# A graph-network kernel: sorting place pairs as one packed word instead of two float planes

## The reference

```python
edge_index = jnp.stack([src, dst])
x = _layernorm(x + _L0_gnn_ref(x, ...gate..., src, dst))           # tanh-gated sum of h[src] into dst
x = _layernorm(x + _L1_gnn_ref(x, edge_index, W1, ..., W2, ...))   # two attention layers, with self loops
x = _layernorm(x + _L2_gnn_ref(x, beta, src, dst))                 # here src is the row index: softmax over
                                                                   # cosine similarities, summed into src
x = _layernorm(x + _L3_gnn_ref(x, edge_index, edge_attr_64, ...))  # relu(x[src] + edge_attr @ Wl + bl) into dst
```

## Time and profile before

| | us |
|---|---|
| median of 3 runs (4032.59 to 4035.59) | 4035.1 |
| the profiled execution | 4035.14 |
| its span in the trace | 4033.3 |
| VectorE (DVE) busy, 5486 instructions | 2409.5 (60%) |
| GpSimd (POOL) busy, 2420 instructions | 2499.7 (62%) |
| TensorE (PE) busy, 5666 instructions | 1601.3 (40%) |
| ScalarE (ACT) busy, 3433 instructions | 1239.6 (31%) |
| part 1 of the sort on VectorE, from 900.47 | to 975.5 |
| part 2, from 1303.39 | to 1373.3 |
| part 3, from 1744.66 | to 1862.95 |

### The profile page before, as it was taken

The page is one execution under the profiler, slowest core; times in us unless marked ns, Lnnn a source line. Parts: engine busy times, 40 slices in busy tenths (PEclk is TensorE's granted clock), DMA queues, the critical chain, the costliest instruction groups (busy, mean ns, idle before and its releaser), DMA issues. The chain is left out here.

```text
span 4033.3 us, 34837 instructions
## 1 busy us (share of the span) xinstructions
PE 1601.3 (40%) x5666; PEld 1320.0 (33%) x5666; DVE 2409.5 (60%) x5486; ACT 1239.6 (31%) x3433; POOL 2499.7 (62%) x2420
## 2 busy tenths in 40 slices
PE   1988989977122156512552000000000277065221
PEld 1888888866122135301220000000000166054221
DVE  5565565549885977678985333348854234443554
ACT  1555555542232255402552222210000144033110
POOL 5777777777701774057602777770377677776777
PEclk9555555555555555556776555555555566566555
DMA  2555556655101244224642555540000155344000
GB/s 56 166 168 165 166 168 184 189 166 141 39 28 34 55 123 128 79 61 112 176 138 84 155 150 150 155 126 0 5 20 20 54 160 158 99 131 115 16 18 17
DMA packets 255330, 421.00 MB, mean 104 GB/s; under 512 B 79304, under 2 KB 86746, under 8 KB 255244
## 3 DMA queue, kind: packets, MB, share of 16 engines
q1 hardware_dynamic: 177932, 348.51, 28.0%
q0 software_dynamic: 77312, 71.64, 9.0%
HBM read 185.35 MB, written 236.81 MB: 105 GB/s over the span
## 5 line engine op out<-in xcount | busy, mean ns | idle before, releaser
L577 PE MATMUL banks<-node_w,x_t 65*125 65x200 f32 x1600 | 551.6, 536 | 0.0
L577 PEld LDWEIGHTS banks<-node_w,x_t 65*125 65x125 f32 x1600 | 514.9, 330 | 4.1
L224 POOL DMA_INDIRECT edge_rows<-x_rows,norm_s x400 | 413.9, 1035 | 144.8 <-issue 125.0
L790 PE MATMUL banks<-ident,cross_in 125*65 125x125 f32 (+4 forms) x26 | 11.2, 430 | 1236.4 <-DVE cross_in L813 848.0
L790 PEld LDWEIGHTS banks<-ident,cross_in 125*65 125x65 f32 (+4 forms) x26 | 3.9, 150 | 1242.1 <-DVE cross_in L813 850.4
L240 POOL DMA_INDIRECT x_rows<-r_x,src_scat_i x200 | 222.1, 1110 | 125.4 <-DVE r_x L2028 63.4
L240 POOL DMA_INDIRECT out_dram<-n_out,scat_i x200 | 222.5, 1112 | 80.1 <-issue 62.0
L620 DVE TENSOR_REDUCE n_var<-n_sq 125x8 f32<-125x512 f32 x125 | 85.6, 686 | 306.4 <-ACT n_sq L634 306.4
L224 POOL DMA_INDIRECT tops<-norm_rows,src_i x200 | 202.6, 1013 | 71.6 <-issue 68.8
L224 POOL DMA_INDIRECT edge_rows<-x_rows,key_i x200 | 199.0, 995 | 77.2 <-issue 60.7
L240 POOL DMA_INDIRECT norm_rows<-edge_rows,scat_i x200 | 205.4, 1027 | 66.6 <-issue 63.3
(11 more groups left out here) (455 smaller groups left out, 5230.2 us busy)
## 6 DMA issues: line engine op xcount, KB each, us to landing
h_rows<-r_h SPq DMA_DIRECT2D x125, 462.0 KB
x_rows<-r_x SPq DMA_DIRECT2D x125, 241.5 KB
x_rows<-r_x SPq DMA_DIRECT2D x125, 224.0 KB
r_x<-x_rows SPq DMA_DIRECT2D x125, 224.0 KB
x_rows<-n_out SPq DMA_DIRECT2D x125, 224.0 KB
n_in<-in_x_dram SPq DMA_DIRECT2D x100, 224.0 KB
x_mixed_edge_rows<-e_dup SPq DMA_DIRECT2D x50, 448.0 KB
n_c<-x_rows SPq DMA_DIRECT2D x100, 224.0 KB
```

The source lines that it names most:

```text
L224: g.indirect_dma_start(out=to[:, j, :], out_offset=None, in_=table, in_offset=bass.IndirectOffsetOnAxis(ap=idx[:, j:j + 1], axis=0)).then_ ...
L577: done = pe.matmul(product[h][:, n // 2, n % 2, :], x_t[u][:, at:at + P], node_w[:, :], start=True, stop=True)
L790: pe.transpose(crossings["bank"][0:cols, 0:rows], frm, ident[0:rows, 0:rows]).then_inc(s_tout, 1)
```

## The change

The key and its companion are packed in one 32-bit word, and the words are sorted as floats, in one plane. The key plus 256 (and plus 768 more from 64768 on) is shifted up by 15 bits, and the companion stands in the low 15 bits. The offsets keep the exponent field clear of its lowest and highest values. Keys whose word has the top bit set sort as negative floats, so the order of the keys is not ascending as a whole, but equal keys stand together and the padding stands in front. At the end the word is taken apart, and the cosine stage reads the last 25000 slots instead of the first. An exchange is one minimum and one maximum. The diff, with its context cut:

```diff
@@ -36,6 +36,8 @@
...
 SORT = 32768
+LOW_BITS, SKIP_AT, SKIP, BASE, PAD_KEY = 15, 64768, 768, 256, 129600
+assert EDGES <= 1 << LOW_BITS and ROWS <= PAD_KEY
 FAR = 1 << 20
@@ -897,7 +899,8 @@
...
         F_BITS = SF.bit_length() - 1
-        k_srt, d_srt = ([o1_t[:, k * SF:(k + 1) * SF] for k in part] for part in ((0, 1), (2, 3)))
+        k_srt = [o1_t[:, k * SF:(k + 1) * SF] for k in range(2)]
+        high, high_i = o1_t[:, 2 * SF:3 * SF], o1_t[:, 3 * SF:4 * SF].bitcast(I32)
         s_srt, ki_srt, di_srt = (t[:, :, :].rearrange("p k f -> p (k f)") for t in (att_tmp, att1, att2))
@@ -921,7 +924,7 @@
...
         PARTS = list(zip(CUTS, CUTS[1:]))
-        held = [t[:, :, :].rearrange("p k f -> p (k f)") for t in (att1, att2)]
+        held = att1[:, :, :].rearrange("p k f -> p (k f)")
@@ -930,33 +933,41 @@
...
         def sort_store_sp(sp):
-            sp.wait_ge(s_sorted, len(PARTS))
+            sp.wait_ge(s_sorted, 1)
             for n, frm in enumerate((ki_srt, di_srt)):
...
             dve.memset(di_srt[:, :], 0)
-            dve.memset(ki_srt[:, :], FAR).then_inc(s_sfill, 1)
+            dve.memset(ki_srt[:, :], PAD_KEY).then_inc(s_sfill, 1)
...
             dve.wait_ge(s_sorting, 64)
-            dve.tensor_copy(d_srt[0][:, :], di_srt[:, :])
-            v.link(dve.tensor_copy(k_srt[0][:, :], ki_srt[:, :]))
+            v.link(dve.tensor_scalar(high, ki_srt[:, :], float(SKIP_AT), float(SKIP), ALU.is_ge, ALU.mult))
+            v.link(dve.scalar_tensor_tensor(high_i, ki_srt[:, :], float(BASE), high, ALU.add, ALU.add))
+            v.link(dve.tensor_single_scalar(high_i, high_i, LOW_BITS, ALU.logical_shift_left))
+            v.link(dve.tensor_tensor(k_srt[0].bitcast(I32), high_i, di_srt[:, :], ALU.bitwise_or))
         def sort_resume_dve(dve):
-            dve.tensor_copy(d_srt[0][:, :], held[1])
-            v.link(dve.tensor_copy(k_srt[0][:, :], held[0]))
-
-        def sort_dve(dve, part, to_k, to_d):
+            v.link(dve.tensor_copy(k_srt[0], held))
+
+        def sort_end_dve(dve):
+            both = k_srt[0].bitcast(I32)
+            dve.tensor_single_scalar(di_srt[:, :], both, (1 << LOW_BITS) - 1, ALU.bitwise_and)
+            v.link(dve.tensor_single_scalar(high_i, both, LOW_BITS, ALU.logical_shift_right))
+            v.link(dve.tensor_scalar(high, high_i, float(SKIP_AT + BASE), -float(SKIP), ALU.is_ge, ALU.mult))
+            dve.scalar_tensor_tensor(ki_srt[:, :], high_i, -float(BASE), high, ALU.add, ALU.add).then_inc(s_sorted, 1)
+
+        def sort_dve(dve, part, to):
             now = 0
...
                 hand_over = n + 1 < len(STEPS) and STEPS[n + 1][0] == "turn"
-                k0, k1, d0, d1 = (t[:, :] for t in (k_srt[now], k_srt[1 - now], d_srt[now], d_srt[1 - now]))
+                k0, k1 = k_srt[now], k_srt[1 - now]
                 if what == "direct":
@@ -966,28 +977,19 @@
...
                     dve.wait_ge(s_tout, crossings["dve"])
-                    dve.tensor_copy(k1, bank[0][:, 0:SF])
-                    done = dve.tensor_copy(d1, bank[0][:, SF:2 * SF])
+                    done = dve.tensor_copy(k1, bank[0][:, 0:SF])
                     now = 1 - now
                 else:
-                    k0, k1, d0, d1 = (t.rearrange("p (n two d) -> p n two d", two=2, d=1 << bit) for t in (k0, k1, d0, d1))
-                    swap = s_srt[:, 0:SF // 2].rearrange("p (n d) -> p n d", d=1 << bit)
-                    diff = s_srt[:, SF // 2:SF].rearrange("p (n d) -> p n d", d=1 << bit)
-                    dve.tensor_tensor(swap, k0[:, :, 0], k0[:, :, 1], ALU.is_gt)
-                    v.link(dve.tensor_tensor(diff, d0[:, :, 1], d0[:, :, 0], ALU.subtract))
-                    v.link(dve.tensor_tensor(diff, diff, swap, ALU.mult))
+                    k0, k1 = (t.rearrange("p (n two d) -> p n two d", two=2, d=1 << bit) for t in (k0, k1))
                     dve.tensor_tensor(k1[:, :, 0], k0[:, :, 0], k0[:, :, 1], ALU.min)
-                    dve.tensor_tensor(k1[:, :, 1], k0[:, :, 0], k0[:, :, 1], ALU.max)
-                    dve.tensor_tensor(d1[:, :, 0], d0[:, :, 0], diff, ALU.add)
-                    done = dve.tensor_tensor(d1[:, :, 1], d0[:, :, 1], diff, ALU.subtract)
+                    done = dve.tensor_tensor(k1[:, :, 1], k0[:, :, 0], k0[:, :, 1], ALU.max)
                     now = 1 - now
...
                     v.link(done)
-            dve.tensor_copy(to_k, k_srt[now][:, :])
-            dve.tensor_copy(to_d, d_srt[now][:, :]).then_inc(s_sorted, 1)
+            v.link(dve.tensor_copy(to, k_srt[now]))
@@ -997,8 +999,7 @@
...
                         part = slice(h * 128, h * 128 + 128)
-                        pe.transpose(bank[0][:, part], k_srt[now][:, part], ident[:, :])
-                        ins = pe.transpose(bank[0][:, SF + h * 128:SF + h * 128 + 128], d_srt[now][:, part], ident[:, :])
+                        ins = pe.transpose(bank[0][:, part], k_srt[now][:, part], ident[:, :])
                     ins.then_inc(s_tout, 1)
@@ -1275,7 +1276,7 @@
...
                 sort_start_dve(dve)
-                sort_dve(dve, PARTS[0], held[0], held[1])
+                sort_dve(dve, PARTS[0], held)
@@ -1637,7 +1638,7 @@
...
                 sort_resume_dve(dve)
-                sort_dve(dve, PARTS[1], held[0], held[1])
+                sort_dve(dve, PARTS[1], held)
                 both = (xa[:, :, 0:D], xa[:, :, 0:D])
@@ -1818,7 +1819,8 @@
...
                 sort_resume_dve(dve)
-                sort_dve(dve, PARTS[2], ki_srt, di_srt)
+                sort_dve(dve, PARTS[2], k_srt[0])
+                sort_end_dve(dve)
                 both = (ha[:, :, 0:D], ha[:, :, D:2 * D])
@@ -1964,8 +1966,8 @@
...
                 sp.wait_ge(s_outside, 1)
-                load_order(sp, SORTED[0, 0:EDGES], s_ordered)
-                sp.dma_start(col_i[:, :], edges_of(SORTED[1, 0:EDGES])).then_inc(s_ordered, 16)
+                load_order(sp, SORTED[0, SORT - EDGES:SORT], s_ordered)
+                sp.dma_start(col_i[:, :], edges_of(SORTED[1, SORT - EDGES:SORT])).then_inc(s_ordered, 16)
                 x3_sp(sp)
```

## The result

The changed kernel takes 3914.8 us, median of 4 runs (3905.9 to 3918.6), against 4033.9 us (4032.0 to 4035.6, 4 runs) before: ratio 0.970, 95% interval 0.969 to 0.972. The forecast was 3913 us. The profiled execution is the shortest of the four, 3905.94 us with a span of 3903.9 us, against 4035.14 and 4033.3 us before. VectorE is busy for 2265.4 us with 4873 instructions, where it had 2409.5 us and 5486.

A forecast was written before the change was run, and what follows sets the result against it. VectorE's serial sort, paced by its count of small instructions, was taken as the bound. Of 161.5 us saved, 26.3 + 23.6 + 72.5 = 122.4 us arrive: 4035.1 - 122.4 = 3912.7, about 3913 us, range 3903 to 3928.

The forecast's parts named there:

- Comparator: VectorE's sort, 120 comparators: seven instructions become min and max, 1.79 to 0.52 us, 1.27 us saved each.
- crossing: Sort parts 2 and 3, 14 times: two transposes instead of four, one PSUM copy instead of two, 0.76 us saved each.
- conversion: Packing at the sort's start and unpacking at its end: +1.0 us and +1.2 us of VectorE work.
- Gate stage: Sort part 1: VectorE saves 44.8 us, 26.3 arrive, 18.5 become a wait for ScalarE's tanh behind its edge projection.
- First attention stage: Sort part 2: VectorE saves 43.0 us, 23.6 arrive, 19.4 are lost to gathers; group 1 starts 21.6 us earlier.
- given back: First attention stage, group boundary: of ScalarE's 2.35 us wait for TensorE, 2.0 us return (bounds 0 to 2.4).
- Second attention stage: Sort part 3: VectorE saves 73.7 us, 72.5 arrive, some 1.2 lost to group 1's gathers.
- A: Rival: all of VectorE's 161.5 us saving arrives, 3874 us; 3%.
- B: Rival: GpSimd's gathers bound the second attention stage too, 5 us lost instead of 1, 3922 us; 12%.
- Rival C: Slower: the new pair order makes the cosine stage's 400 gathers longer; 4073 us at 0.4 us more each; 3%.
- D: Rival: no change, 4035 us, since the stages do not wait for VectorE's sort; 2%.
- The port: Attention stages: rule that two-input VectorE instructions slow GpSimd's gathers; judged already at their floor beside comparators, sum unchanged.

The follow-up runs named there:

- spread: Changed kernel with 18 of the 25 edge projection rounds ahead of the first tanh, the other 7 carried by the next chunks; 3901.4 us, 0.967 of before.
- groups: Changed kernel with columns cut at other chunks (4, 2, 5, 5, 5, 4 instead of 4, 5, 5, 5, 4, 2); 3892.9 us, 0.966 of before.
- before_again: The kernel before the change, unaltered, run again in the first slow job; 6200.3 us, 0.999 of before.
- after_third: The changed kernel, unaltered, run again in the second slow job; 6024.6 us, 0.974 of before.
- twice_3b: Changed kernel with two extra VectorE instructions in each of part 3's 54 comparators, in the second slow job; 6064.4 us, 0.982 of before.

## Why the prediction was right

**Comparator, crossing, conversion.** 0.53 us for 0.52. The crossing: 0.34 us for the copy and 0.43 us less of waiting, 0.77 for 0.76. The conversion at the start is 1.69 us for the 0.62 us of the copies, +1.1 (said +1.0); at the end 1.61 for 0.41, +1.2 as said. VectorE reached group 0 of the second attention stage 73.0 us earlier, counted from the stage's start (1744.02 - 1691.31 against 1862.95 - 1737.20); said 73.7.

**Gate stage.** 26.3 us forecast for the tanh's result; measured 26.2 (115.4 us after the first sort instruction before, 89.1 after), and 0.6 more by the stage's end. The wait is 19.9 us, its old 1.73 among them, so 18.2 were lost; said 18.5. That the projection is what this wait is for is shown by spread, which moved seven of its rounds and took the wait away. The projection kept its place: its last copy comes 86.9 us after the first sort instruction in both kernels.

**First attention stage, the step that was mis-sized.** Group 0 started at 42.7 us (said 43.3): a gather landed after 2.5 us, not 3.0. Group 1 started 20.2 us earlier, not 21.6, inside the bounds: its last gather was issued 96.1 us into the stage where the forecast had 94.5. Its 40 gathers took 1.40 us each, the forecast had 1.35. So the slow pace of gathers under chunks holds for more of the 40 than was taken. The waits before groups 0 and 1, 7.8 and 14.4 us, make 22.1 us in all, where the prediction had some 9 and 13. (Its bounds for this step aren't quite of one kind: the slow one, 1396.3, lets the last gather land in 2.5 us, the fast one in 3.0. It doesn't matter here.) And the 2.0 us "given back" did not come: groups 1 to 5 start 20.2, 20.1, 20.0, 20.1 and 20.4 us earlier, and the stage ends 20.3 earlier. ScalarE's rows tell why:

```profile
1372.60 0.18 ACT L1743 COPY own<-banks 125x12 f32<-125x12 f32 x1
...
1380.05 0.17 ACT L1743 COPY own<-banks 125x12 f32<-125x12 f32 x1 [6.05 <-PE banks L1697]
1380.11 0.49 ACT L1744 COPY r_h<-banks 125x396 f32<-125x396 f32 x1
...
1381.75 0.28 DVE L1521 COPY dens_selfs<-head 125x40 f32<-125x40 f32 x2 [9.16 <-ACT norm_d L1568]
```

The first copy behind the group boundary no longer waits for TensorE, as said. But VectorE stands for 9.16 us behind the exponentials, where it stood for 9.03 us before, and ScalarE's time went into the wait before its next copy (6.05 us; before, 3.47). From the group's first instruction to the one behind the exponentials VectorE takes 12.4 us before (1415.03 to 1427.39) and 12.5 after (1369.27 to 1381.75). So the 2.35 us weren't on the path, and of the 3.3 us by which this stage was missed this term has 1.9: 2.0 us were put down as given back, and 0.1 came. The other 1.4 us are the pace of the 40 gathers, less the earlier landing.

**Second attention stage.** Right to 0.3 us, but by luck: two errors cancel. The wait before group 1 took 2.6 us, not 1.2, and that group starts 69.6 us earlier where 72.5 were forecast; then the later groups start 70.7, 72.0, 71.4 and 72.2 us earlier, and the stage ends 72.2 earlier. Some 2.6 us came back in the stage where I expected none. What gives them back isn't shown.

**Rivals.** A (all arrives) falls by the waits of 19.9, 7.8 and 14.4 us. B had the size of the first attention stage partly right (18.7 with nothing given back; 20.3 measured), but not its own claim: the second lost no 6 us. Rival C falls by the page's row of the cosine stage's gathers by key, 987 ns each after and 995 before, and by all 400, which take 517.7 us from the first to the last after and 519.1 before:

```profile
L226 POOL DMA_INDIRECT edge_rows<-x_rows,key_i x200 | 197.5, 987 | 77.8 <-issue 60.7
```

D falls by the time.

**The port.** The rule weighed in the prediction (the Trainium skill, SBUF — State Buffer, Who interferes with whom) shows little beside the comparators. The 32nd gather of the first attention stage is issued 40.2 us after its start, and 40.3 us before the change. That alone says nothing, since instructions with two SBUF inputs follow one another as fast in either kernel (7 in 1.79 us, 2 in 0.53). But beside after's comparators of part 2 most gathers take 0.95 us and a few 1.03 to 1.07, and beside a waiting VectorE they take 0.95. Under the chunks it is otherwise. GpSimd's rows of after, one gather beside a VectorE that waits and one beside a wide multiplication, with that VectorE row:

```profile
1309.31 0.95 POOL L226 DMA_INDIRECT edge_rows<-x_rows,norm_s  x1 [0.30 <-issue]
...
1327.77 1.62 POOL L226 DMA_INDIRECT edge_rows<-x_rows,norm_s  x1 [0.30 <-issue]
```

```profile
1327.61 2.00 DVE L1546 TENSOR_TENSOR x_t<-edge_rows,pen_reach 125x512 f32<-125x512 f32 x2
```

In after, of the gathers behind 800 us, 304 had a wide tensor_tensor with both inputs in SBUF (125x512) beside them for more than half of their time and took 1.15 us on average; 538 beside an idle VectorE took 0.95, 401 beside other VectorE work 0.99. The trace agrees with the rule there, and the 1.40 us of a gather under chunks, the pace that was put too low, goes with it. It is a coincidence in time in one trace, not an experiment: no run took these multiplications away.

**Cosine and message stage.** The forecast had no change. The profiled execution was 11.3 us shorter in them, and it lies 9 us below the median of its kernel; the stages of the other three executions aren't known. Over the six kernels with the changed sort in ordinary jobs the cosine stage lasts 992.0 to 1000.7 us and the message stage 838.6 to 845.4; there is one profile of before there, 1003.0 and 843.2. What the change could touch in the cosine stage is the 400 gathers: the last is issued 526.2 us into the stage before, and 523.5 to 528.7 us in the six. So the 6.7 us lie behind the gathers, in a stretch that differs by 13 us among the six themselves. Whether 2 or 3 us of the stage belong to the change stays open, and nothing in these rows is for it.

## What to carry to other kernels

When the work on a stage's longest chain shrinks, the saving ends at the next thing that was ready just in time, so write down for each stage when that thing is ready: here the end of another engine's queue (19.9 us) and the landing of a group of gathers (14.4 us). A row that shows an engine waiting isn't a promise of time given back: ask who waits for that engine, and until when (2.35 us that nobody missed). After such a change the waits it leaves are cheap to look at, and moving what they wait for was worth another 27 us here by the profiled spans, 37 by the medians (3914.8 to 3877.9).

## What the runs showed of the hardware that I had not expected

In two jobs every kernel took some 53% longer (6206 and 6186 us for before), and only in stretches: the gate stage kept its 394 us, while the first attention stage went from 441 to 645, and what lies ahead of the sort from 900 to 1823. By the numbers on record the second of these jobs had the same chip as spread and groups, which ran there at the ordinary pace, so the slowness isn't shown to belong to a chip. VectorE's timelines there, before_again and then after_third, with the idle time ahead of each instruction:

```profile
2307.06 0.29 DVE L976 TENSOR_TENSOR att_tmp<-o_t 128x128 f32<-128x128 f32 x1 [4.65 <-remote]
...
2309.16 0.29 DVE L978 TENSOR_TENSOR att_tmp<-att_tmp 128x128 f32<-128x128 f32 x1 [1.61 <-remote]
2310.56 0.29 DVE L979 TENSOR_TENSOR o_t<-o_t 128x128 f32<-128x128 f32 x1 [1.11 <-DVE att_tmp L978]
...
2316.16 0.29 DVE L976 TENSOR_TENSOR att_tmp<-o_t 128x128 f32<-128x128 f32 x1 [4.70 <-remote]
```

```profile
2234.50 0.29 DVE L984 TENSOR_TENSOR o_t<-o_t 128x128 f32<-128x128 f32 x1 [2.31 <-remote]
2234.71 0.28 DVE L985 TENSOR_TENSOR o_t<-o_t 128x128 f32<-128x128 f32 x1
2237.30 0.29 DVE L984 TENSOR_TENSOR o_t<-o_t 128x128 f32<-128x128 f32 x1 [2.31 <-issue]
```

Each instruction lasts as long as ever, 0.28 to 0.29 us. But a comparator of seven instructions has a period of 9.1 to 9.8 us (1.79 elsewhere), one of four, in twice_3b, one of 4.9 to 5.6 us (3007.09 to 3011.99 is 4.9), and one of two 2.1 to 2.8 us (0.53). There the sort's time goes by the number of its instructions, each worth some 1.1 to 1.4 us, and the change saves 167 and 161 us where it saves 119 elsewhere (ratios 0.973 and 0.974).

The slow stretches are those in which GpSimd issues gathers or scatters, and they set in some 40 us late and end some 30 us late. Windows of before_again, two ahead of the sort and two in part 3 of it, then the first window in before (stretch, length, busy us and instructions of PE, PEld, DVE, ACT, POOL):

```profile
500.00:600.00 100.00, 12.68 (x40) 10.70 (x40) 9.56 (x20) 7.69 (x20) 73.77 (x71) 0.50 0.13 27
1200.00:1300.00 100.00, 90.17 (x307) 85.69 (x306) 57.03 (x122) 56.57 (x153) 0.00 (x0) 0.50 0.54 166
3040.00:3100.00 60.00, 1.11 (x4) 0.71 (x4) 11.13 (x43) 0.00 (x0) 45.38 (x48) 0.50 0.24 53
3145.00:3186.00 41.00, 2.23 (x8) 1.43 (x8) 36.38 (x150) 0.00 (x0) 0.00 (x0) 0.50 0.00 0
```

```profile
500.00:600.00 100.00, 90.18 (x305) 85.75 (x305) 58.68 (x124) 56.18 (x152) 73.63 (x73) 0.50 0.56 168
```

In the same kind of work VectorE gets through 20 instructions in 100 us beside 71 gathers and through 122 with none beside it; in the ordinary job it gets through 124 beside 73. In part 3 the last gather is issued at 3114.29, and from 3143.25 on a comparator takes 1.79 us again. The gate stage's sort starts at 1823.0, GpSimd's last gather for that stage is issued at 1125.6, and the sort isn't slowed. In the first attention stage the gathers begin at 2197.8, and the comparators keep 1.79 us until 2239. The exception is the last stretch, the 200 scatters of the output: it takes 283 us as in the ordinary job. The gathers themselves aren't slower than elsewhere: the 72nd of the first attention stage is issued 90.6 us into it (92.0 in the ordinary job). By what path GpSimd's work holds back the others there, and why only in these two jobs, isn't shown by any row: no releaser stands beside most of the waits ("issue", "remote").
